# Count groups in bursts, output additions that wait for other experts only, and the order of the general path

## What is computed

```python
# 6250 nodes of 256 features, 200000 edges sorted by target, 16 edge types, 8 experts
h   = layernorm(x)
msg = h[src] + relvectors[edge_type]
red = segment_sum(msg, dst, 6250)              # one row per target node
x   = x + gru_cell(red, h, w_ih, w_hh, b_ih, b_hh)
xf  = layernorm(x)
mask = top-2 of (xf @ Wg + bg), as 0/1         # 2 experts per node
y   = gelu(xf @ W1[e] + b1[e]) @ W2[e] + b2[e] # 256 -> 512 -> 256
x   = x + sum over experts e of mask[:, e] * y[e]
```

## Time and profile before

| | |
|---|---|
| median of 3 runs | 1694.0 us (1689.6 to 1695.6) |
| profiled execution | 1692.36 us, its span 1690.5 us |
| PE busy | 1397.3 us (83%) |
| DVE busy | 1075.3 us (64%) |
| POOL busy | 1033.4 us (61%) |
| ACT busy | 708.9 us (42%) |

### The profile page before, as it was taken

The page is one execution under the profiler, slowest core; times in us unless marked ns, Lnnn a source line. Parts: engine busy times, 40 slices in busy tenths (PEclk is TensorE's granted clock), DMA queues, the critical chain, the costliest instruction groups (busy, mean ns, idle before and its releaser), DMA issues.

```text
span 1690.5 us, 39892 instructions
## 1 busy us (share of the span) xinstructions
PE 1397.3 (83%) x14228; PEld 1172.8 (69%) x14228; DVE 1075.3 (64%) x3958; ACT 708.9 (42%) x1538; POOL 1033.4 (61%) x948
## 2 busy tenths in 40 slices
PE   1269999999999999999888989885465999989990
PEld 1247878887877778877777778674464977777770
DVE  7767676776676786679788788954454544444440
ACT  7333334343444444434333332222133766556660
POOL 2277667677766677577777776777712444445452
PEclk8568999999999999999899898786776999999995
DMA  9676334454544444444454443448413454555446
GB/s 312 168 221 202 113 94 121 129 151 118 144 131 132 131 129 115 118 141 132 141 147 129 133 126 102 118 122 319 123 43 99 81 84 78 84 79 85 79 74 172
DMA packets 136165, 220.58 MB, mean 130 GB/s; under 512 B 27761, under 2 KB 101046, under 8 KB 134688
## 3 DMA queue, kind: packets, MB, share of 16 engines
q0 software_dynamic: 63872, 123.12, 30.3%
q1 hardware_dynamic: 72096, 94.84, 18.3%
HBM read 169.05 MB, written 57.76 MB: 134 GB/s over the span
## 4 chain that ended last, share of the span: by engine, by line
PE 38%; DMA 20%; DVE 16%; POOL 10%; issue 7%; ACT 5%; SPq 1%; DVEq 1%; POOLq 0%; ACTq 0%
DMA out_rows<-yo,xrows 13%; PE P L1573 12%; PE P L1538 11%; POOL out_rows L659 5%; PE P L1521 4%; DMA raw<-in_L_ffn_W_dram 4%; POOL ring L614 4%; PE P L1483 3%; DVE cone L1072 3%; DVE lone L1071 2%; PE P L1525 2%; DMA ring<-h_table,idx 2%; ACT amat L716 2%; PE P L1474 1%; POOL expert_rows L623 1%
## 5 line engine op out<-in xcount | busy, mean ns | idle before, releaser
L614 POOL DMA_INDIRECT ring<-h_table,idx x728 | 724.8, 996 | 341.4 <-issue 255.3
L716 ACT ACTIVATE amat<-P 128x300 f16<-128x300 f32 (+3 forms) x608 | 240.4, 428 | 618.6 <-PE P L1525 611.3
L1538 PE MATMUL P<-hs,amat 128*126 128x256 f16 (+4 forms) x2646 | 329.3, 282 | 0.0
L1538 PEld LDWEIGHTS P<-hs,amat 128*126 128x126 f16 (+4 forms) x2646 | 300.4, 139 | 4.9
L659 POOL DMA_INDIRECT out_rows<-yo,xrows x112 | 177.4, 1584 | 206.3 <-DMA out_rows<-yo,xrows 163.4
L1521 PE MATMUL P<-cone,lone 128*128 128x294 f16 (+3 forms) x840 | 217.8, 295 | 62.6 <-DVE cone L1072 44.0
L1072 DVE TENSOR_SCALAR cone<-iota,comb 128x294 f16<-128x294 f16 (+3 forms) x840 | 262.9, 316 | 0.0
L1071 DVE TENSOR_SCALAR lone<-iota,slo 128x128 f16<-128x128 f16 x840 | 222.8, 266 | 2.9 <-PE P L1521 2.4
L623 POOL DMA_INDIRECT expert_rows<-xrow,slots x100 | 122.3, 1223 | 70.4 <-DVE slots L1201 40.8
L1751 PE MATMUL P<-xh,w_all 128*128 128x256 f16 x896 | 157.8, 274 | 7.6 <-issue 7.6
L1764 PE MATMUL P<-w_all,gh 128*128 x896 | 149.8, 273 | 0.7 <-DVE gl L1412 0.6
(11 more groups left out here) (230 smaller groups left out, 2676.2 us busy)
## 6 DMA issues: line engine op xcount, KB each, us to landing
raw<-in_L_ffn_W_dram SPq DMA_DIRECT2D x32, 512.0 KB
xrows<-expert_rows SPq DMA_DIRECT2D x56, 257.0 KB, 2.7
ring<-h_table,idx POOLq DMA_INDIRECT x728
w_parts<-parts SPq DMA_DIRECT2D x16, 512.0 KB
w_all<-w_parts SPq DMA_DIRECT2D x8, 1024.0 KB
h_in<-h_table SPq DMA_DIRECT2D x25, 250.0 KB
x<-in_x_dram SPq DMA_DIRECT2D x25, 250.0 KB
out_rows<-x SPq DMA_DIRECT2D x25, 250.0 KB
```

The source lines that it names most:

```text
L614: nc.gpsimd.indirect_dma_start(out=ring[:, r, j, :], out_offset=None, in_=h_dram, in_offset=bass.IndirectOffsetOnAxis(ap=idx[:, slot, g * ...
L716: nc.scalar.activation(amat[:, b % 2, :, s * aw:(s + 1) * aw], P[2 + g % 2][:, 0:HIS * aw].rearrange("p (h w) -> p h w", w=aw), ACT.Copy). ...
L1538: nc.tensor.matmul(to, amat[:, b % 2, hi, 0:used], hs[:, hi, part * D:(part + 1) * D], start=(hi == 0 and part == 0), stop=False)
```

## The change

In the count groups, PE takes up to two groups at once (`bursts_of(h)`: pairs of groups with k < 4, in order; a group of k = 4 stands alone). All waits of a burst stand ahead of its first matmul; the large matmuls of both groups follow, then the small ones. The first burst stands where the early groups stood; the others follow one by one, and the half step's piece of the big product is cut into as many parts as there are bursts and dealt out between them. ACT takes the groups of the first burst early and the rest late. DVE's order is as before (`len(mine) // 2` early).

In the expert stage there are two semaphores for landed additions, one for even and one for odd blocks. DVE computes once, in `first_blocks()`, for every block how many even and odd blocks belong to earlier experts; POOL loads these two numbers into registers and waits for them, in place of all earlier blocks. A block of padding rows still waits for all earlier blocks. DVE's and SP's waits use the semaphore of the block's own parity.

In the general path, the bands follow the tiles' order of the plan; none of it runs on these inputs.

```diff
+def bursts_of(h):
+    out = []
+    for g in groups_of(h):
+        if out and len(out[-1]) == 1 and GROUPED[g][2] < GC and GROUPED[out[-1][0]][2] < GC:
+            out[-1].append(g)
+        else:
+            out.append([g])
+    return out
...
SP
-                    sp.wait_ge(y_added, 32 * (b - XR + 1))
+                    sp.wait_ge(y_added[b % 2], 32 * ((b - XR) // 2 + 1))
...
POOL
+            pool.wait_ge(firsts_ready, 1)
+            def earlier(b):
+                return [pool.value_load(firsts[0:1, n * BLOCKS + b:n * BLOCKS + b + 1], min_val=32, max_val=16 * BLOCKS)
+                        for n in range(min(b, 2))]
+            before = earlier(0)
             for b in range(BLOCKS):
                 pool.wait_ge(y_out, b + 1)
-                if b:
-                    pool.wait_ge(y_added, 32 * b)
+                for n in range(min(b, 2)):
+                    pool.wait_ge(y_added[n], before[n])
                 for j in range(2):
                     nc.gpsimd.indirect_dma_start(
...
-                        in_=yo[:, b % 2, j, :], in_offset=None, compute_op=ALU.add).then_inc(y_added, 16)
+                        in_=yo[:, b % 2, j, :], in_offset=None, compute_op=ALU.add).then_inc(y_added[b % 2], 16)
+                if b + 1 < BLOCKS:
+                    before = earlier(b + 1)
...
ACT
-                    mine = groups_of(h)
-                    for g in mine[:len(mine) // 2]:
+                    bursts = bursts_of(h)
+                    for g in bursts[0] if bursts else []:
                         move_group(g)
...
-                    for g in mine[len(mine) // 2:]:
+                    for g in groups_of(h)[len(bursts[0]):] if bursts else []:
                         move_group(g)
...
DVE
+            def first_blocks():
+                n_b = nb[:, NE:2 * NE]
+                shape = [1, BLOCKS, NE]
+                blocks = rowc[0:1, NE + NE * NE:NROWC]
+                of, earlier, dead = brow[:, 0, :], brow[:, 6, :], brow[:, 7, :]
+                after(nc.vector.tensor_tensor(len_[:, :, :], le[:, :, :], n_b.unsqueeze(1).to_broadcast(shape), ALU.mult))
+                nc.vector.tensor_scalar(dead, of, float(NE) - 0.5, None, ALU.is_ge)
+                after(nc.vector.tensor_reduce(earlier, len_[:, :, :], AX, ALU.add))
+                after(nc.vector.tensor_tensor(dead, dead, blocks, ALU.mult))
+                after(nc.vector.tensor_tensor(earlier, earlier, dead, ALU.max))
+                nc.vector.tensor_scalar_add(brow_i[:, 0:BLOCKS], earlier, 1.0)
+                after(nc.vector.tensor_copy(brow_i[:, BLOCKS:2 * BLOCKS], earlier))
+                after(nc.vector.tensor_scalar(brow_i[:, :], brow_i[:, :], 1, 5, ALU.logical_shift_right, ALU.logical_shift_left))
+                nc.vector.tensor_scalar(firsts[:, :], brow_i[:, :], 32.0, None, ALU.max).then_inc(firsts_ready, 1)
...
-                    dve.wait_ge(y_added, 32 * (b - 1))
+                    dve.wait_ge(y_added[b % 2], 32 * (b // 2))
...
             low_rows(1)
+            first_blocks()
             low_g(0)
...
PE
+            def head_burst(groups):
+                if groups[-1] >= 2:
+                    pe.wait_ge(a_moved, groups[-1] - 1)
+                pair, at, k, aw, seq = chunk_of(groups[-1])
+                if pair + 1 > seen[0]:
+                    seen[0] = pair + 1
+                    pe.wait_ge(a_windows, pair + 1)
+                pe.wait_ge(a_ready, seq + k)
+                for g in groups:
...                                                    # k matmuls lone x cone of group g
+                for g in groups:
...                                                    # k matmuls tone x wone of group g
+                    ins.then_inc(a_group, 1)
...
-                    for g in mine[:len(mine) // 2]:
-                        head_group(g)
+                    bursts = bursts_of(h)
+                    if bursts:
+                        head_burst(bursts[0])
...
-                    if h in PIECE_AT:
-                        head_piece(*PIECE_AT[h])
-                    for i in stage_of(h, 10):
-                        rank(i)
-                    for g in mine[len(mine) // 2:]:
-                        head_group(g)
+                    of = max(len(bursts), 1)
+                    for m in range(of):
+                        if h in PIECE_AT:
+                            head_piece(*PIECE_AT[h], m, of)
+                        if m == 0:
+                            for i in stage_of(h, 10):
+                                rank(i)
+                        if m + 1 < len(bursts):
+                            head_burst(bursts[m + 1])
```

More of the change, by code:

```diff
@@ L132 @@
 ACOLS = HEADC + LIVE + WIN
-assert BW * WIN <= ACOLS and HEAD % 2 == 0
+assert HEAD % 2 == 0
 def plan():
@@ L173, with band_runs, band_column @@
 ENDS = max(BEGIN[-1] + 12, HALVES + 2)
+def band_runs():
+    bands = []
+    for b in range(BANDS):
+        runs = []
+        for t in sorted(ORDER[b * BT:b * BT + BT]):
+            if runs and t == runs[-1][0] + runs[-1][1]:
+                runs[-1][1] += 1
+            else:
+                runs.append([t, 1])
+        bands.append([[t, n, -(-n * T // WIN)] for t, n in runs])
+    most = max(sum(w for _, _, w in runs) for runs in bands)
+    for runs in bands:
+        runs[-1][2] += most - sum(w for _, _, w in runs)
+    return bands, most
+RUNS, BW = band_runs()
+assert BW * WIN <= ACOLS
+def band_column(i):
+    at = 0
+    for t, n, w in RUNS[i // BT]:
+        if t <= ORDER[i] < t + n:
+            return at + T * (ORDER[i] - t)
+        at += w * WIN
 FREE_TILE = min(i for i in range(TILES) if BEGIN[i] > ADDED_AT[-1])
@@ L433, in gnn_ffn_kernel @@
         x_in = [sem(f"x_in{n}") for n in range(XR)]
+        y_added = [sem(f"y_added{n}") for n in range(2)]
         def table_whole(eng):
@@ L1337, in general @@
[L1337 to L1340 removed]
+                            done = 0
+                            for n, (first, _, windows) in enumerate(runs):
+                                with dve.Fori(0, windows) as w:
+                                    window((b * STEPS + s) * BW + (w + done), s, s * per_step + w + (moved + done + n),
+                                           w * WIN + done * WIN)
+                                done += windows
+                                after = runs[(n + 1) % len(runs)][0]
+                                dve.wait_ge(g_ramp, s * per_step + (moved + done + n))
+                                nc.vector.tensor_scalar_add(ramp_w[:, :], ramp_w[:, :],
+                                                            float(T * (after - first) - WIN * windows)).then_inc(g_ramp, 1)
@@ L1535, in head_piece @@
                 to = P[1 + 3 * (b % 2)][0:used, 0:D]
-                for hi in range(HI * n // pieces, HI * (n + 1) // pieces):
+                for hi in range(HI * (n * of + m) // (pieces * of), HI * (n * of + m + 1) // (pieces * of)):
                     for part in range(2):
@@ L1539, in head_piece @@
                                          start=(hi == 0 and part == 0), stop=False)
-                if n == pieces - 1:
+                if n == pieces - 1 and m == of - 1:
                     for part in range(PARTS):
```

94 lines of the change are left out of this document (48 added, 46 removed).

## The result

The changed kernel took 1666.2 us in the median of 4 runs (1662.9 to 1670.6), the kernel before 1692.9 beside it (4 runs, 1689.6 to 1695.6): a ratio of 0.984, 95% interval 0.981 to 0.986. That is 1.6% less, clear of the noise and inside the range, but 18 us short of the forecast. Its profiled execution, the slowest of the four, took 1670.6 us with a span of 1668.7.

A forecast was written before the change was run, and what follows sets the result against it. No single engine bounds the whole: POOL's addition chain paces the expert stage; PE, DVE and POOL share the graph stage. -44 - 24 + 18 + 4 = -46 us: profiled 1692.4 becomes 1646, median 1648; own range 1622 to 1668, with rivals 1618 to 1676.

The forecast's parts named there:

- Expert stage, -44 us: Expert stage: blocks of one expert no longer wait for landing, period falls to PE's 5.68 us, gain 44 us.
- The rival in which POOL is the bound: Expert stage: POOL needs 5.9 us per block, gain 31 in place of 44, time 1661 us; chance 0.10.
- The one in which additions don't overlap: Expert stage: landing sets the pace, period stays 6.5 us, time 1692 us; chance 0.04.
- k=1 bursts, -24 us: Graph stage, half steps 0 to 101: bursts save 47 us of PE time, half taken as gain, 24 us.
- a rival of the k=2 stretch: PE's first k=2 bursts: waits of 1.2 us, each with 0.8 us of slow clock behind, 1734 us; chance 0.05.
- PE's idle issue before the small loads below 10 us: Graph stage: sign to look for, PE's idle "issue" before small weight loads falls from 57.6 to below 10 us.
- PE is already ahead of its waits: Graph stage: the 0.23 us gap is pipeline depth, only the bursts' losses stay, 1672 us; chance 0.10.
- k=2 bursts, +18 us: Graph stage, half steps 101 to 144: first bursts wait for a second group that DVE builds late, 18 us lost.
- k=4, +4 us: Graph stage, half steps 145 to 159: each of 32 groups waits for all four chunks, 4 us lost.
- Pieces, 0 within 3 us: Graph stage: splitting the pieces moves no work off PE, 0, within 3 us either way.
- `first_blocks`, 0: Nine small added DVE instructions, some 3 us, fall where DVE waits for ACT: 0, at most 0.5 us.
- the 25 that the prediction named as its limit: Stretch to 1286 us: prediction counts as wrong if it moves by more than 25 us either way.

The follow-up runs named there:

- f1: Changed kernel's expert stage with the graph stage of the kernel before, on the usual chip: 1656.1 us, 0.975 of the kernel before.
- f0: The changed kernel itself, run again on the usual chip: 1666.0 us, 0.981 of the kernel before.
- f2: Changed kernel with VectorE building early all groups of TensorE's first burst, on the usual chip: 1662.6 us, 0.979 of the kernel before.
- f3: Changed kernel with each piece whole ahead of the second burst, on the usual chip: 1672.7 us, 0.985 of the kernel before.
- e4: Changed kernel with VectorE building the first burst's groups early and pieces whole, on a slow chip: 2145.6 us, 0.988 of the kernel before.
- e2: Changed kernel with VectorE building early all groups of TensorE's first burst, on a slow chip: 2125.1 us, 0.976 of the kernel before.
- set 2: Runs f0, f1, f2 and f3 beside the kernel before on one chip with the usual time; the kernel before took 1699.8 us there.
- e1: Changed kernel's expert stage with the graph stage of the kernel before, on a slow chip: 2135.8 us, 0.984 of the kernel before.
- g2: Changed kernel with TensorE waiting before each large matmul for its own chunk, on a slow chip: 2123.5 us, 0.975 of the kernel before.
- g4: Changed kernel gathering three of four chunks per upper gathered group, output not valid, on a slow chip: 1908.1 us, 0.874 of the kernel before.

## Why the prediction was right in its sign, and 18 us short

**Expert stage, -44 us: right, and so was its mechanism.** Measured 45.2 us in the profiles, 43.7 in f1's time. The period is 5.68 us and PE's, the copy starts 318.6 us after the first addition (320 was said), padding takes 6.4 us a block (6.46), and delays at an expert's first block are made good. POOL's loads are cheaper than I took: 0.29 + 0.15 us each [L705 above] against 0.50 + 0.20, two of each in the 2.25 us before a block's first addition. With 5.68 - 2.25 = 3.43 us for the additions and 0.9 for the loads, POOL needs 4.3 us of the 5.68, before its wake-up. The floor of about 0.6 us that the Trainium skill, "DMA: Bandwidth & Descriptors", section "Latency and other measured facts", gives for a register load is not seen here: the 109 loads took 0.28 to 0.31 us. That the first instance at L444 took 0.50 was the poorer guide. The rival in which POOL is the bound is refuted by the 2.25 us of waiting for `yo`. The one in which additions don't overlap is refuted too: a block's second addition starts 1.87 us after its first and lands 4.1 us later, at 5.97 us, and the next block starts after 5.68; 39 of the 55 later blocks start before the one before has landed, where none did in the kernel before. The 49 us named as the most don't follow from the rows: 55 periods of 5.68 us in place of 6.51 are 46.

**k=1 bursts, -24 us: the step that failed.** The size per pair was nearly right (0.45 us said, 0.47 measured at 294 columns; a gain of 0.19 for 0.21), and PE's work fell. The step from work to time failed: "I take half". Over half steps 0 to 101 the bursts were worth 636.9 against 640.7 us, 3.8 us (f0 against f1), and in the profile of the changed kernel they cost 2.6 (641.2 for 638.6 before). The gain is real from 17 to 60 (8.9 us) and given back behind it. Two things show for it. ScalarE's copies: TensorE's waits for `amat` from 60 to 101 went from 36 waits of at most 1.1 us (9.9 us in all) in f1 to 14 of at most 2.8 us (14.2 us) in f0, since a burst needs both banks. And the clock: 41.0 us at the lower level in that stretch where f1 has 17.1. I had priced the slow clock behind a wait only as a rival of the k=2 stretch. That the waits for both banks brought the lower clock is read from these rows; no run varied the one without the other.

**"PE's idle issue before the small loads below 10 us": wrong, also in sign.** It rose from 57.6 to 79.0 us. With the waits gone 324 loads still stand idle some 0.24 us (79.0 / 324), so the wait was not what held them. Groups that stand alone in their burst settle it: at 245 columns and the upper clock the small matmul starts 0.199 us after the large one without a wait (29 groups) and 0.209 with one (185 groups in the kernel before). The wait costs 0.01 us, so single groups gain nothing like the 0.10 that I gave each. The rival "PE is already ahead of its waits" named this, and its 1672 us is nearer to the result than my 1648. It is right that the 0.23 us is not the wait, and wrong that only losses stay, since a pair did become 0.19 us shorter. By these rows the gap still stands once in a burst, behind the second large matmul (0.22 us of the 0.47); what is saved is the gap of the first group, since a large matmul follows it and not its small one. That the saving per pair came out is in part luck. The rule of the Trainium skill that I set aside there ("TensorE: Matmul & The Clock Gate", section "Step-by-step: what each phase is for": loads are pulled ahead of matmuls in flight, if the row groups don't conflict or the load goes to the background weight buffer) is of no help either. In the trace the large matmul's load starts ahead of it (609.13 for 609.24 us), while the small one's starts only with its own matmul (both 609.43), with or without a wait. Which of the two conditions fails there, no run shows.

**k=2 bursts, +18 us: right in size, wrong in what it hangs on.** 101 to 144 became 16.4 us longer (17.1 in f0 against f1), and the waits for `cone` 17.9 us (35.6 for 17.7; I had said 40 for 20). I put it to VectorE building the second group late. Built early, it made 2.2 us of difference (f2), so that the size came out is luck. Whether TensorE's place for the second group or the wait for all four chunks makes the loss is open: argued for the place is that the last chunk of the burst is ready at the same time either way, and the piece waits behind it. Against it, waits per chunk would let three of four large matmuls run beside the builds, 0.4 us at the upper clock and 0.8 at the lower, at each of the 18 waits: by estimate 7 to 14 us of the 17. No run on a usual chip has tried either. The run of slow matmuls behind each wait, 0.8 us of it in my rival, is part of it: 61.4 us at the low level for 36.9 in f1, by an estimate from the difference 12 us of lost work at half speed.

**k=4, +4 us: right** (96.3 and 97.2 for 93.6). **Pieces, 0 within 3 us: too little**; dividing them saves 6.8 us (f3 against f0), and leaving it out cost 20 us on a slow chip too (e4 against e2). **`first_blocks`, 0: right**; nothing of it shows before the first addition, whose delay of 22.8 us is, within 1 us, the sum of the stretches before it.

The sum was -44 - 24 + 18 + 4; the runs say about -45 - 1 + 17 + 3, which is 1693 - 26 = 1667. The term that is missing is the one for the k=1 bursts. The terms come from single profiles and are good to a few us: on the chip of set 2 the medians give -43.7 for the additions and +9.9 for all of the graph stage, where -1 + 17 + 3 would be +19. The graph stage, forecast at -2 us in all, moved by +22.8 in the profile, close to the 25 that the prediction named as its limit; a result of 1666 lies in the forecast's own range of 1622 to 1668 by 2 us only. On the usual chip the version to keep is the one with the additions alone, 1656.1 us beside 1666.0.

## What to carry to other kernels

When instructions are moved together, their saving is busy time; it becomes time only if what feeds the group can deliver all of it at once, so ask of every burst which engine makes its last operand and what independent work now stands behind the wait. Look at the longest wait of TensorE and not at their sum alone: from 60 to 101 its clock was low for 41.0 us in place of 17.1 where its waits for `amat` had become fewer (14 for 36) and longer (2.8 us for 1.1). A wait for the landing of a DMA that protects only some pairs of blocks is worth a register load (0.44 us here) to decide which.

## What the runs showed of the hardware

**Chips on which engines stand still while GpSimd issues its indirect DMAs.** The two slow chips did not differ in the expert stage (318.4 us of e1 beside 318.3 of f1) or in the time of a transfer: the 4 KB packets of the gathers took 0.22 us in e1 and 0.23 in f1. What they have is gaps of up to 15.7 us on ScalarE, VectorE and TensorE that the profile puts down to nothing in the kernel. All engines of e1 in order of time, cut to one of them:

```profile
711.03 0.28 PE L1618 MATMUL P<-cone,lone 128*128 128x245 f16 x1 [0.43 <-issue]
...
711.41 1.29 POOL L660 DMA_INDIRECT ring<-h_table,idx  x1 [0.30 <-issue]
713.00 0.95 POOL L660 DMA_INDIRECT ring<-h_table,idx  x1 [0.30 <-issue]
714.25 0.95 POOL L660 DMA_INDIRECT ring<-h_table,idx  x1 [0.30 <-issue]
715.51 0.95 POOL L660 DMA_INDIRECT ring<-h_table,idx  x1 [0.31 <-issue]
716.77 0.95 POOL L660 DMA_INDIRECT ring<-h_table,idx  x1 [0.30 <-issue]
717.81 0.40 ACT L773 ACTIVATE amat<-P 128x250 f16<-128x250 f32 x1 [6.83 <-remote]
718.26 0.39 PE L1618 MATMUL P<-cone,lone 128*128 128x245 f16 x1 [6.85 <-issue]
```

ScalarE and TensorE stand still until the row of gathers is done. Counted over these three engines from 100 to 1800 us, waits above 2.5 us that end in "issue" or "remote" are 158 in e1 (942 us), 164 in g2 (909 us) and 2 in f1 (6 us), none of them in the expert stage. 91% of that time in e1 and g2 lies beneath indirect DMAs that GpSimd is issuing for gathers and for the scatter to the experts' rows (with the 0.3 us behind each), where 64 and 65% of all time from 200 to 1700 us does; beneath gathers alone it is 75%, for 56 and 57%. With a quarter of the gathers left out (g4) there are 110 (542 us), and the kernel is 215 us faster than g2. That the gaps hang on the gathers is shown; whether on their issue or on their traffic, and by what path, is not, and neither is what sets these two chips apart.

**Additions of neighbouring blocks overlap without loss.** The addition of 1618.76 lands some 4.1 us later at the median, the next block's first one starts at 1621.79; 39 of 55 blocks start so. All landed in 3.7 to 5.3 us, and their issue kept its median of 1.56 us. Rows of two additions never meet in one place while both are in flight, since only blocks of one expert overlap and an expert has a node once; what happens where they meet was not tried.
